# Second attention of an adaLN/MoE block: query and key stacks laid out over both partition halves, and four-head units scored and masked on two row groups of TensorE

## The reference, cut to what matters

```python
# 16 heads of 8 dimensions, 512 positions, 8 batches
q, k, v = shape(x @ w_q.T), shape(x @ w_k.T), shape(x @ w_v.T)     # rotary on q and k
scores = einsum('bhqd,bhkd->bhqk', q, k)
scores = scores + einsum('bhqd,qkd->bhqk', q, rel)                  # rel_emb[clip(k - q, -32, 32) + 32]
scores = where(causal, scores, NEG_INF)
attn = softmax(scores)
ctx = einsum('bhqk,bhkd->bhqd', attn, v) + einsum('bhqk,qkd->bhqd', attn, rel)
```

## Time and profile before

| | |
|---|---|
| runs (three) | 1816.12 us median, 1816.05 to 1820.46 |
| profiled execution | 1806.88 us, span in the trace 1805.1 us |
| granted TensorE clock, mean | 0.967 of full speed |
| PE busy | 1604.0 us (89%), 37004 matmul records, 37004 weight loads |
| DVE, ACT, POOL busy | 1076.1, 700.8, 848.0 us |
| first attention | about 38 to 788 us |
| second attention | about 938 to 1612 us |

### The profile page before, as it was taken

How to read it: one execution, slowest core, us unless ns; L and a number is a source line. 1 busy time by engine, 2 the same in 40 slices (tenths; PEclk the granted TensorE clock), 3 DMA queues, 4 the chain that set the end, 5 groups by cost and what they waited for, 6 DMA issues and landing times.

```text
span 1805.1 us, 81110 instructions
## 1 busy us (share of the span) xinstructions
PE 1604.0 (89%) x37004; PEld 1258.8 (70%) x37004; DVE 1076.1 (60%) x2271; ACT 700.8 (39%) x1135; POOL 848.0 (47%) x802
## 2 busy tenths in 40 slices
PE   6789999999999988888997898999999899978993
PEld 4566666666666666677885676777777777768993
DVE  3657676767688865538426466665656666544334
ACT  2344444443434433345542243433333343434441
POOL 2556555656555546527767153424233243015552
PEclk9999999999999999999998899999999999989997
DMA  9800000000000000043254424323241413026886
GB/s 301 270 23 3 6 5 3 8 3 8 3 8 3 8 5 17 14 138 42 63 103 52 91 46 94 67 62 81 47 92 44 89 46 91 18 75 171 232 226 189
DMA packets 102062, 128.52 MB, mean 71 GB/s; under 512 B 12533, under 2 KB 80761, under 8 KB 100488
## 3 DMA queue, kind: packets, MB, share of 16 engines
q1 hardware_dynamic: 81112, 103.52, 21.7%
q0 software_dynamic: 15808, 16.93, 4.8%
q10 hardware_dynamic: 4800, 2.89, 0.6%
HBM read 91.70 MB, written 54.07 MB: 81 GB/s over the span
## 4 chain that ended last, share of the span: by engine, by line
PE 59%; DVE 17%; POOL 11%; issue 7%; ACT 3%; DMA 2%; POOLq 0%; ACTq 0%; SPq 0%; DVEq 0%
PE psum L1204 55%; DVE colmax L1950 3%; POOL rope_b L2249 2%; DVE ctx_sum L1962 2%; POOL rope_a L2247 2%; DVE colmax L2059 2%; DVE rowmax L1957 2%; DVE raw L1907 2%; POOL arena L2299 1%; ACT prob L1660 1%; PE psum L1538 1%; POOL added_rows L2324 1%; POOL ffw L2263 1%; DVE rowmax L2067 1%; ACT arena L1677 1%
## 5 line engine op out<-in xcount | busy, mean ns | idle before, releaser
L1204 PE MATMUL psum<-arena 128*32 128x32 f32 (+8 forms) x10296 | 571.6, 251 | 27.8 <-issue 24.8
L1204 PEld LDWEIGHTS psum<-arena 128*32 128x32 f32 (+3 forms) x10296 | 451.0, 126 | 105.5 <-issue 66.5
L1677 ACT ACTIVATE arena<-psum 128x1024 f32<-128x1024 f32 (+1 forms) x192 | 169.3, 882 | 304.5 <-PE psum L1204 300.6
L1204 PE MATMUL psum<-prob,ffw 128*32 128x128 f32 x5120 | 206.1, 280 | 26.4 <-DVE rowmax L1957 24.2
L1692 ACT COPY ctx_sum<-psum 128x384 f32<-128x384 f32 x128 | 61.2, 478 | 400.3 <-PE psum L1204 359.0
L2059 DVE TENSOR_REDUCE colmax<-psum 128x256 bf16<-128x768 f32 (+2 forms) x160 | 178.2, 1114 | 57.1 <-PE psum L1204 54.1
L1950 DVE TENSOR_REDUCE colmax<-psum 128x512 bf16<-128x2048 f32 (+2 forms) x96 | 168.0, 1750 | 64.9 <-PE psum L1204 64.9
L2299 POOL TENSOR_TENSOR arena<-ctx_sum 128x256 f32<-128x256 f32 x128 | 94.6, 739 | 215.4 <-DVE ctx_sum L1962 203.8
L1204 PEld LDWEIGHTS psum<-prob,ffw 128*32 128x32 f32 x5120 | 139.1, 111 | 73.1 <-DVE rowmax L1957 54.1
L2067 DVE TENSOR_REDUCE rowmax<-psum 128x2 bf16<-128x256 f32 (+1 forms) x192 | 97.8, 509 | 137.4 <-PE psum L1204 136.5
L1660 ACT ACTIVATE prob<-psum 128x2048 f32<-128x2048 f32 (+3 forms) x128 | 158.6, 1239 | 10.9 <-PE psum L1204 10.0
(11 more groups left out here) (248 smaller groups left out, 2553.0 us busy)
## 6 DMA issues: line engine op xcount, KB each, us to landing
sent<-in_empty SPq DMA_DIRECT2D x9, 2112.0 KB, 41.5
arena<-in_down_pack SPq DMA_DIRECT2D x39, 320.0 KB, 3.3
arena<-qk_parts SPq DMA_DIRECT2D x96, 128.0 KB
arena<-in_up_pack SPq DMA_DIRECT2D x39, 258.0 KB, 3.1
q_copies<-arena SPq DMA_DIRECT2D x32, 256.0 KB
prob<-q_copies SPq DMA_DIRECT2D x128, 64.0 KB
qk_parts<-arena SPq DMA_DIRECT2D x16, 384.0 KB, 4.4
arena<-sent SPq DMA_DIRECT2D x39, 132.0 KB, 2.9
```

The lines of the kernel that those rows point to most:

```text
L1204: return pe.matmul(o, lhsT, rhs, start=start, stop=stop, skip_group_check=True)
L1677: act.activation(probs_of(i)[:, :, h0 * P:(h0 + nh) * P], slot(n)[:, 0:(i + 1) * W].rearrange("p (j c) -> p j c", c=W), ACT.Exp, scale=HD1 ...
```

## The change

The stacks get a new layout: both batches of a pair stand beside each other along the free axis (index b mod 2), and the partition halves hold the heads instead: of a group's four heads the first two stand at rows 0 to 47, the other two at rows 64 to 111. Each stack DMA is split into two, one for each half, with pieces of two heads (1024 bf16) in place of rows of sixteen. In a four-head unit the two halves write two different PSUM banks (`halves`), so the mask is four matmuls of 64 rows and 128 columns, the scores alternate between the row groups, each band matmul becomes two of half the columns (one for each bank), and the shift of query block 1 takes both key blocks in one matmul of 256 columns. Two-head units keep their place in PSUM; their mask becomes two matmuls of 64 rows. `causal` and `neg_half` go, `neg_ident` takes the place of the latter in the first attention too. DVE's reduction and ACT's cast and exponential of four-head units get one more dimension in their access patterns, with the same number of elements.

```diff
+        later_keys = sb("later_keys", [P, 2, P], BF16)
...
-        q_st = carve([H1 * S // 2], restart=True).bitcast(BF16).rearrange("p (h s) -> p h s", h=H1)
-        k_st = carve([H1 * S // 2]).bitcast(BF16).rearrange("p (h s) -> p h s", h=H1)
+        q_st = carve([H1 * S // 2], restart=True).bitcast(BF16).rearrange("p (z h s) -> p z h s", z=2, s=S)
+        k_st = carve([H1 * S // 2]).bitcast(BF16).rearrange("p (z h s) -> p z h s", z=2, s=S)
...
+        def halves(n, blocks):
+
+            return psum[:, 2 * (n % 2):2 * (n % 2) + 2, 0:blocks * 2 * P].rearrange("p z (j c) -> p z j c", j=blocks)
...
-            return 16 * 6 * (b // 2 + 1)
+            return 16 * 6 * 2 * (b // 2 + 1)
...
-                        row = 64 * (b % 2) + HD1 * r
-                        sp.dma_start(stack[row:row + HD1, :, :],
-                                     parts_dram[b, which, :, pp, :].rearrange("d (h s) -> d h s", h=H1)).then_inc(
-                                         d_stack[b % 2][what], 16)
+                        for z in range(2):
+                            row = HQ * z + HD1 * r
+                            sp.dma_start(stack[row:row + HD1, b % 2, :, :].rearrange("d (g h) s -> d g (h s)", g=NG),
+                                         parts_dram[b, which, :, pp, :].rearrange("d (g z c) -> d g z c", g=NG, z=2)[
+                                             :, :, z, :]).then_inc(d_stack[b % 2][what], 16)
...
-                                         neg_half[rows, :].unsqueeze(1).to_broadcast([HQ, 2, HQ]), start=(half == 0))
+                                         neg_ident[rows, rows].unsqueeze(1).to_broadcast([HQ, 2, HQ]), start=(half == 0))
...
-                        r0 = 64 * (b % 2)
                         w.wait_ge(prob1_ready, n - 1)
                         w.wait_ge(hid_done, FC * UNITS0)
                         w.wait_ge(d_stack[b % 2]["key"], stack_value(b))
                         w.wait_ge(d_stack[b % 2]["query"], stack_value(b))
-                        mm(slot(n)[:, i * W:(i + 1) * W], ident_bf[:, :],
-                           causal[:, :].unsqueeze(1).to_broadcast([P, nh, P]), True)
+                        row_groups = (0, 1) if nh == GRP else (h0 // 2,)
+                        for half in range(2):
+                            for z in row_groups:
+                                rows = slice(HQ * z, HQ * (z + 1))
+                                block = halves(n, i + 1)[:, z, i, :] if nh == GRP else slot(n)[:, i * W:(i + 1) * W]
+                                mm(block.rearrange("p (a q) -> p a q", a=2)[:, :, HQ * half:HQ * (half + 1)],
+                                   later_keys[rows, half, :], neg_ident[rows, rows].unsqueeze(1).to_broadcast([HQ, 2, HQ]),
+                                   start=(half == 0))
                         for j in range(i + 1):
-                            for a in range(nh):
-                                h = GRP * g + h0 + a
-                                mm(slot(n)[:, j * W + a * P:j * W + (a + 1) * P],
-                                   k_st[r0:r0 + ROWS, h, j * P:(j + 1) * P], q_st[r0:r0 + ROWS, h, i * P:(i + 1) * P],
-                                   start=(j * W // BANK < i * W // BANK and j * W % BANK == 0 and a == 0))
+                            for a in range(2):
+                                for z in row_groups:
+                                    rows = slice(HQ * z, HQ * z + ROWS)
+                                    if nh == GRP:
+                                        to, opens = halves(n, i + 1)[:, z, j, a * P:(a + 1) * P], False
+                                    else:
+                                        to = slot(n)[:, j * W + a * P:j * W + (a + 1) * P]
+                                        opens = j * W // BANK < i * W // BANK and j * W % BANK == 0 and a == 0
+                                    mm(to, k_st[rows, b % 2, 2 * g + a, j * P:(j + 1) * P],
+                                       q_st[rows, b % 2, 2 * g + a, i * P:(i + 1) * P], start=opens)
                         w.wait_ge(d_qx[g % 2], 16 * QG * ((NG * b + g) // 2 + 1))
                         for r in range(4):
                             for q, c, before in band_round(r, i):
                                 keys = slice(QUAD * q, QUAD * (q + 1))
-                                ins = mm(chunk(slot(n)[keys, (i - before) * W:(i - before + 1) * W], c).rearrange(
-                                             "p h (t j) -> p h t j", t=QG),
-                                         band_slice(NCH * before + c)[:, keys],
-                                         qx[:, g % 2, h0:h0 + nh, :].rearrange("p h (t x j) -> p h t x j", t=QG, j=QC)[
-                                             :, :, :, i * NCH + c, :], False)
+                                for z in row_groups:
+                                    block = (halves(n, i + 1)[keys, z, i - before, :] if nh == GRP else
+                                             slot(n)[keys, (i - before) * W:(i - before + 1) * W])
+                                    ins = mm(chunk(block, c).rearrange("p h (t j) -> p h t j", t=QG),
+                                             band_slice(NCH * before + c)[:, keys],
+                                             qx[:, g % 2, 2 * z:2 * z + 2, :].rearrange(
+                                                 "p h (t x j) -> p h t x j", t=QG, j=QC)[:, :, :, i * NCH + c, :], False)
                         ins.then_inc(scored1, 1)
...
-                        for j in range(0, i + 1, BANK // W):
-                            nj = min(BANK // W, i + 1 - j)
+                        for j in range(0, i + 1, 2):
+                            nj = min(2, i + 1 - j)
                             for a in range(nh):
                                 for q in range(QG):
                                     keys = slice(QUAD * q, QUAD * (q + 1))
-                                    ins = mm(slot(n)[keys, j * W:(j + nj) * W].rearrange("p (j c) -> p j c", j=nj)[
-                                                 :, :, a * P:(a + 1) * P],
+                                    blocks = (halves(n, i + 1)[keys, a // 2] if nh == GRP else
+                                              slot(n)[keys, j * W:(j + nj) * W].rearrange("p (j c) -> p j c", j=nj))
+                                    ins = mm(blocks[:, :, a % 2 * P:(a % 2 + 1) * P],
                                              rowmax[:, n % 2, a:a + 1].to_broadcast([P, QUAD]),
                                              neg_ident[:, :].unsqueeze(1).to_broadcast([P, nj, P]), False)
                         ins.then_inc(shifted1, 1)
...
-                        act.copy(colmax[:, n % 2, :], slot(n)[:, 0:BANK]).then_inc(colmax1_act, 1)
+                        act.copy(colmax[:, n % 2, :].rearrange("p (z c) -> p z c", z=2),
+                                 halves(n, 1)[:, :, 0, :]).then_inc(colmax1_act, 1)
...
-                        act.activation(probs_of(i)[:, :, h0 * P:(h0 + nh) * P],
-                                       slot(n)[:, 0:(i + 1) * W].rearrange("p (j c) -> p j c", c=W), ACT.Exp,
-                                       scale=HD1 ** -0.5).then_inc(prob1_ready, 1)
+                        if nh == GRP:
+                            to = probs_of(i).rearrange("p j (z c) -> p z j c", z=2)
+                            there = halves(n, i + 1)
+                        else:
+                            to = probs_of(i)[:, :, h0 * P:(h0 + nh) * P]
+                            there = slot(n)[:, 0:(i + 1) * W].rearrange("p (j c) -> p j c", c=W)
+                        act.activation(to, there, ACT.Exp, scale=HD1 ** -0.5).then_inc(prob1_ready, 1)
...
-                        dve.tensor_reduce(colmax[:, n % 2, 0:W],
-                                          slot(n)[:, 0:(i + 1) * W].rearrange("p (j c) -> p c j", c=W),
-                                          AX.X, ALU.max).then_inc(colmax1_dve, 1)
+                        if u["nh"] == GRP:
+                            dve.tensor_reduce(colmax[:, n % 2, :].rearrange("p (z c) -> p z c", z=2),
+                                              halves(n, i + 1).rearrange("p z j c -> p z c j"),
+                                              AX.X, ALU.max).then_inc(colmax1_dve, 1)
+                        else:
+                            dve.tensor_reduce(colmax[:, n % 2, 0:W],
+                                              slot(n)[:, 0:(i + 1) * W].rearrange("p (j c) -> p c j", c=W),
+                                              AX.X, ALU.max).then_inc(colmax1_dve, 1)
```

More of the change, by code:

```diff
@@ L80 @@
 TABLE2 = NT * E + 2 * NT + TILES_OF + TILES
-ARENA = 28912
+ARENA = 28832
 class Waits:
@@ L167, in shape_constants @@
         "ident": np.eye(P, dtype=np.float32),
-        "causal": np.stack([np.where(p[:, None] <= p[None, :], 0.0, NEG)] + [
-            np.where(p[:, None] % HQ + HQ * half >= p[None, :], 0.0, -NEG) for half in range(2)], 1).astype(np.float32),
```

(16 more changed lines are left out.)

## The result

The changed kernel takes 1834.95 us (median of 4 runs, 1827.82 to 1837.31) against 1816.09 (4 runs, 1811.24 to 1820.46): ratio 1.0108, 95% interval 1.0085 to 1.0131. It is slower by 1.1 to 1.3%, 19 and 23 us between the medians; the forecast was 17.

What follows compares the result with a forecast made beforehand. PE was taken as the bound, by its array and by fetching blocks of 256 instructions. Second attention +21 us (array -11, 13.5 more blocks, p 0.45), stacks -4: +17 us, 1833 us; range 1810 to 1854.

Steps and rivals of the forecast that it cites:

- Two limits, blocks of 256: PE in the second attention: besides array work, each block of 256 instructions costs at least the time to bring the next.
- The floor: Second attention: shortest time of a block of 256 PE instructions bounded by its supply, 3.46 to 3.73 us.
- Array time, -11 us: Second attention: mask, scores, shift and band together save 0.35 us a group over 32 groups; -4 to -18 us.
- the formula: Second attention's time as 177.4 x (4.07 - (1 - p) x 0.35) us, p being the share of supply-bound blocks.
- the band: Four-head units: 32 matmuls of 64 columns become 64 of 32, +0.11 us each unit, between 0 and +0.21.
- Instructions, +3456, 13.5 blocks: PE in the second attention: 1728 more matmul records, each with a load, 177.4 blocks in place of 163.9.
- The share p of supply-bound blocks: Second attention: share of blocks that keep their 4.07 us, 0.27 before, taken as 0.45 after; stage 688 us, +21.
- The stacks, -4 us: Stack DMAs in 2 KB pieces in place of 16 KB rows delay instruction packets less: -4 us, at most 14.
- DVE, the other stages, start-up: 0: DVE and ACT keep their element counts, other stages keep their time: 0, up to +4 us if DVE's extra dimension shows.
- A: Rival: instruction supply does not bind further in the second attention and the array gain arrives, 1805 us; chance 0.16.
- B: Rival: p stays at 0.27 and the stacks give 7 us or more, +3 or less, 1819 us; chance 0.13.
- C: Rival: the second half of each band pair holds up all strips behind it, +83 us, about 1880 us; chance 0.05.

Runs made afterwards that it cites:

- e7: Kernel before plus 3456 repeated weight loads, 18 in each shift of the second attention: 1.0225 of the kernel before, +41 us.
- e6: Changed kernel without the second of each pair of band matmuls in four-head units: 0.9837 of the kernel before, 1791.3 us.
- e8: Changed kernel with the second attention's shift as one full-array matmul in place of four strips, timed a second time: 0.9923 of the kernel before.
- e5: The changed kernel timed again in a later session, nothing else altered: 1.0134 of the kernel before, 1842.6 us.
- e9: Changed kernel with the full-array shift, and one full-array mask matmul of 256 columns in two-head units: 0.9862 of the kernel before, 1787.9 us.
- e10: Kernel before with the second attention's shift on the full array in place of four strips: 0.9912 of the kernel before.
- e11: Kernel before with only the change's stack DMAs, 24 per batch in 2 KB pieces in place of 12 in 16 KB: 0.9990 of the kernel before.
- e7 early: Kernel before plus 3456 repeated weight loads, 27 in each transposition of maxima of the first attention: 1.0016 of the kernel before, +3 us.
- e1: Kernel before plus 3456 PE waits on semaphore values already reached: 1.1218 of the kernel before in the second attention, 1.2156 in the first.

## Why the prediction was right, and which terms were not

**Two limits, blocks of 256.** Right: e7, e6 and e8 each move instructions and array time apart, and the time follows the blocks. That "issue" is the fetching of instructions, which the prediction took from the 256, the 64 bytes and the packets of the earlier trace rows, is borne out by the packets' own times: PE goes on 1.4 us after its block's packet has landed. The floor is where the prediction put it: the two shortest lengths that recur are 3.47 and 3.75 us, beside its 3.46 and 3.73.

**Array time, -11 us.** The sign was right, the size was not. Group time fell by 0.05 to 0.14 us, not 0.35: -2 to -4 us, which in the formula is 177.4 x 0.55 x (0.35 - 0.31) = 4 us of the result. By part: mask -0.09 (forecast -0.10), scores -0.23 and -0.11 (-0.23, -0.12), shift -0.02 (-0.02), and the band +0.21 and +0.17 where I took +0.11. Its upper end was right: two trains of 32 short loads, 0.75 against 0.49 us. Columns halved from 64 to 32 made the same 32 records only 29% shorter (0.49 to 0.35), so splitting costs nearly a whole train. The two-head mask, taken as 0, costs 0.02 in each of 128 units, since the change of form ahead of it grew by more than the mask shrank (maxima to mask 0.11 to 0.21, mask to scores 0.20 to 0.12). The Trainium skill's "TensorEngine Tiling (Array Packing)", section "Instruction Overhead", by which the doubled train would take, as an estimate, near twice 0.49 us, is further off than my value. The trace lies between. The prediction's +0.38 for it is over my own +0.11 and not over "now", for twice 0.49 is +0.49. The sum's other end was off by one as well: with the band at +0.21 it is -5 us, not -4.

**Instructions, +3456, 13.5 blocks.** Exact: 38732 records.

**The share p of supply-bound blocks.** I took 0.45, from 0.27 before. Counted as there, by the gaps of the waits, it is 92 / 177 = 0.52, and 0.55 in e5. Putting in what was measured, work and waits per block of (635 - 3) / 177.4 = 3.56 us, 0.31 less than 3.87, and 0.52: 177.4 x (4.07 - 0.48 x 0.31) = 696 us, +29. Measured: 697.4 against 667, +30, and +29 between the means of the two executions of after's stage (705.7) and the three of before's (676.7). So on the change the formula gives back the stage, with a share that was read only afterwards; the share had been set too low, which is 177.4 x 0.07 x 0.31 = 4 us. It does not carry far: with the work, blocks and shares of the windows of e9 and e10 it gives 678 and 693 us where 653 and 671 were measured. The 0.20 us between its 3.87 and 4.07 are before's own issue time spread over all blocks, and do not go as the gaps go.

**The stacks, -4 us.** No relief is seen in e11: the gaps (56, 46 us) and the issue time are those of before or more, though its timing does not exclude 4 us. How much the stacks delay instruction packets at all stays open: of the changed kernel's gap time about 52 of 94 us lie within 2.5 us of a stack's issue, but so does 46% of the stage's whole time.

**DVE, the other stages, start-up: 0.** Right. Only my remark that the waits for DVE's column maxima would shrink was wrong (31.4 to 31.2).

So the +17 us had three errors of about 4 us each (array, p, and the relief by the stacks), all in one direction, and the stage's +29 shows them. That the medians' +19 and +23 came out nearer to +17 is in part luck.

**Rivals.** A (the array gain arrives) is refuted by the change: the kernel became slower, and the issue time doubled. With the instruction count near that of before, saved array time does arrive (e6, which leaves out half of the band: 0.984). B (balance) would have needed p at 0.27. C (strips block each other) fell with the band: 0.75 us of loads, not 1.9. What A was to be decided by held as well: of the 282 blocks with a gap at both ends in seven of these kernels one was under 3.4 us, at 3.35. The Trainium skill's "Advanced Engine Details and Errata", section "ISA Cache", has lines of 256 instructions, and the trace agrees; of several such lines in advance on TensorE this trace shows nothing: a block of 2.5 us of work between two others still took 3.46.

## What to carry to other kernels

Before splitting matmuls to fill more of the array, divide PE's instructions (matmuls and loads together) by 256 and the stage's time by that: where a block is near 4 us, as here (4.07 before), count an added instruction at its share of a block (here about 3 us for 256, e7) and not at its columns. Blocks of 6.8 us of work paid nearly nothing (e7 early), and at 4.6 us the gaps were all but gone (e10). Where long "issue" gaps on PE stand 128 + 128 records apart, look for the form with the fewest instructions, even if its columns cost more: four strips with the same data are one full-array matmul, and 0.2 us of form changes bought 24 instructions (e8, e9). The same edit paid 34 to 41 us in one kernel and 16 in the other, so it has to be priced in the kernel that it goes into.

## What was unexpected of the hardware

- An event wait on PE whose value was reached long ago came 0.106 us after the one before it (e1), a repeated 32-column weight load about 1 ns where blocks are long (e7 early: 3 us for 3456).
- Blocks with a gap at both ends do not take any length. 3.47, 3.74 or 3.75, 4.02, 4.29, 4.57, 4.84, 5.12 and 5.39 us are 210 of the 282, steps of 0.27 us. The two values of the earlier trace rows and the windows above lie on this grid. What ticks at 0.27 us is open.
- A change of array form costs 0.1 us wherever it stands: moved from behind the mask to ahead of it, it stayed the same size, and two more per unit in e8 added 0.2.
- Issue time was as long with stacks in 2 KB pieces as in 16 KB ones (33.3 and 32.0 us, e11).
- The packet of the next block of 256 instructions started only 1.24 us (median) after PE had entered the block before, and PE went on 1.42 us after it had landed.
